# Edge scores by digit masks and one maximum, with one 16-plane load of edge numbers and three score buffers

## The reference

```
xp    = layernorm(x) @ W                       # 3125 x 1024, as 4 heads of 256
a_src = sum over a head's 256 of xp * att_src  # 3125 x 4
a_dst = sum over a head's 256 of xp * att_dst  # 3125 x 4
e     = leaky_relu(a_src[src] + a_dst[dst], 0.2)   # one row of 4 per edge
alpha = softmax of e over the edges of one dst
out   = relu(sum over a dst's edges of xp[src] * alpha + bias)
x     = x + out;   x = x + expert_layer(layernorm(x))
```

## Time and profile before

| | |
|---|---|
| median of 3 runs | 2159.19 us (2158.75 to 2162.96) |
| span of the profiled execution | 2296.1 us |
| what lies around that span | not shown |
| PE busy, its weight loads | 1959.2 us (85%), 1318.7 us (57%) |
| VectorE busy | 1470.6 us (64%) |
| ScalarE, GpSimd busy | 1137.3 us (50%), 768.2 us (33%) |
| DMA | 490.15 MB, mean 213 GB/s |
| score stage | 332 to 483 us |

### The profile page before, as it was taken

How to read it: one execution, slowest core, us unless ns; L and a number is a source line. 1 busy time by engine, 2 the same in 40 slices (tenths; PEclk the granted TensorE clock), 3 DMA queues, 4 the chain that set the end, 5 groups by cost and what they waited for, 6 DMA issues and landing times. The chain is left out here.

```text
span 2296.1 us, 53233 instructions
## 1 busy us (share of the span) xinstructions
PE 1959.2 (85%) x14846; PEld 1318.7 (57%) x14847; DVE 1470.6 (64%) x4341; ACT 1137.3 (50%) x2499; POOL 768.2 (33%) x943
## 2 busy tenths in 40 slices
PE   6999977667878888888888589983899999999997
PEld 4666545645766667777667455652454445555553
DVE  7988859987666666666666699867543443443333
ACT  4444421113666666676666566654543443443332
POOL 1020000022555555555555232321233333333332
PEclk9999976568999999999999889995899999999999
DMA  7444544403988888888888677746646556644542
GB/s 272 134 143 136 172 131 172 186 0 114 312 281 291 286 299 287 294 296 287 287 298 294 235 249 240 228 142 234 233 169 249 212 167 239 221 160 171 176 162 80
DMA packets 135664, 490.15 MB, mean 213 GB/s; under 512 B 16900, under 2 KB 17108, under 8 KB 133410
## 3 DMA queue, kind: packets, MB, share of 16 engines
q0 software_dynamic: 95568, 334.62, 43.5%
q1 hardware_dynamic: 31954, 125.15, 15.1%
q10 hardware_dynamic: 8064, 29.36, 3.7%
HBM read 419.17 MB, written 81.17 MB: 218 GB/s over the span
## 5 line engine op out<-in xcount | busy, mean ns | idle before, releaser
L1130 PE MATMUL main_ps<-rows,O 128*128 128x256 f16 x4992 | 619.2, 283 | 125.7 <-DVE acc L1066 66.3
L1113 ACT ACTIVATE O<-O,pk 128x128 f16<-128x128 f16 x1664 | 502.9, 387 | 246.1 <-DVE O L1083 203.5
L1130 PEld LDWEIGHTS main_ps<-rows,O 128*128 128x128 f16 x4992 | 480.9, 102 | 217.9 <-issue 72.8
L1052 POOL DMA_INDIRECT rows<-projected,idx x416 | 395.5, 951 | 325.2 <-PE small_ps L1135 202.9
L1087 DVE TENSOR_SCALAR O<-O,pk 128x128 f16<-128x128 f16 x1664 | 314.6, 273 | 15.0 <-issue 0.2
L1837 PE MATMUL x_h<-w_p,gram 128*128 x1344 | 307.1, 386 | 18.4 <-ACT gram L1787 7.6
L1852 PE MATMUL x_o<-w_p,gram 128*128 x1344 | 308.0, 379 | 1.4 <-ACT gram L1806 1.4
L1886 PE MATMUL pj_ps<-gram,xsT 128*125 128x512 f16 x1200 | 271.1, 385 | 8.8 <-ACT xsT L402 5.5
L1837 PEld LDWEIGHTS x_h<-w_p,gram 128*128 128x128 f16 x1344 | 131.6, 99 | 171.6 <-issue 31.5
L1886 PEld LDWEIGHTS pj_ps<-gram,xsT 128*125 128x125 f16 x1200 | 163.2, 139 | 104.7 <-ACT xsT L402 8.6
L1083 DVE TENSOR_SCALAR O<-iota,pk 128x128 f16<-128x128 f16 x416 | 109.4, 263 | 164.9 <-PE small_ps L1135 124.1
(11 more groups left out here) (346 smaller groups left out, 2538.9 us busy)
## 6 DMA issues: line engine op xcount, KB each, us to landing
w_f<-in_L_ffn_W_dram SPq DMA_DIRECT2D x14, 2048.0 KB
b_t<-in_L_ffn_b_dram ACTq DMA_DIRECT2D x56, 512.0 KB
projected_f<-xp_f POOLq DMA_DIRECT2D x25, 500.0 KB, 3.7
projected<-xp POOLq DMA_DIRECT2D x25, 500.0 KB, 4.6
out_dram<-n_x SPq DMA_DIRECT2D x25, 500.0 KB
x_after_gnn_normed<-PK POOLq DMA_DIRECT2D x25, 500.0 KB, 9.1
xt<-in_x_dram SPq DMA_DIRECT2D x24, 512.0 KB, 3.3
n_own<-projected_f SPq DMA_DIRECT2D x24, 512.0 KB, 13.0
```

The source lines that it names most:

```text
L1052: pool.indirect_dma_start(out=rows[:, 4 * p + k, :, :].rearrange("k n d -> k (n d)"), out_offset=None, in_=xp_d[:, :], in_offset=bass.Indi ...
L1113: ins = act.activation(O[:, k, 1 + HEADS + h, :], O[:, k, 0, :], ACT.Copy, scale=pk[:, p, k, w:w + 1])
L1130: pe.matmul(main_ps[:, h * C:(h + 1) * C], O[:, k, 1 + HEADS * a + h, :], rows[:, 4 * p + k, b, h * C:(h + 1) * C], start=first and h % 2 ...
```

## The change

A source is now split in base 112: `high = src // 112` (28 values, `HI`) and `low = src % 112`. `high` itself is split into `tens = high // 7` and `ones = high % 7`. Of the 128 rows of a one-hot column, 112 stand for `low`, 8 for `tens` and 8 for `ones`. The matrix that PE multiplies with (`terms`, 128 rows, 28 x 4 columns, two parts) holds the node terms in rows 0 to 111, and in the 16 rows below them a mask: 0 where a column's digit is the row's, -65504 elsewhere. The product is thus the edge's term in the right place, and a number near -65504 or lower in the 27 others, and one maximum over the 28 places finds it.

- `edge_numbers` makes three number rows (`low`, `tens`, `ones`) beside the local dst; SP stores them as 16 planes of DRAM: `low` 14 times, then `tens` and `ones`. A chunk's load copies each plane to 8 partitions (`load_numbers`), and VectorE compares each partition with its own number `src_row`.
- `digit_mask` (at block 16) makes `src_row`, a shifted identity and the mask, in 18 VectorE instructions (3 for the identity, 4 for `src_row`, 9 for the mask's values, 2 copies). After the last block PE puts the mask and the shifted node terms into `spread_ps` (about 50 small matmuls), and VectorE copies it to `terms`.
- `high_one_hots` and the turned row `hiT` are gone, and so are `pick` and the product at L790.
- There are three buffers of score sums; PE waits until the reduction of the group three before is done, where it waited for the product of the group two before.
- All eight chunks are written out on PE.

```
-HI = -(-NODES // P)
+LOW, TENS, DIGITS = 112, 7, 8
+HI = -(-NODES // LOW)
+MASK = -65504.0
...
+        def load_numbers(sp, lo, dl, vs, done):
+            sp.dma_start(lo, numbers_d[:, vs, :].rearrange("n v k -> n (v k)").unsqueeze(1).broadcast_to([P // DIGITS, DIGITS, CHUNK * P])).then_inc(done, 16)
+            sp.dma_start(dl, dloc_d[vs, :].partition_broadcast(P)).then_inc(done, 16)
...
-                            sp.dma_start(lo_d.rearrange("(p r) n -> p (r n)", r=4), rowV[:, 0, :]).then_inc(s_vstore, 16)
+                            lows = LOW // DIGITS
+                            sp.dma_start(numbers_d[0:lows].rearrange("n (p r) k -> p n (r k)", r=4),
+                                         rowV[:, 0, :].unsqueeze(1).broadcast_to([VP, lows, ROW4])).then_inc(s_vstore, 16)
+                            sp.dma_start(numbers_d[lows:].rearrange("n (p r) k -> p n (r k)", r=4), rowV[:, 2:4, :]).then_inc(s_vstore, 16)
...
-                        dve.scalar_tensor_tensor(fV[:, 2, :], fV[:, 1, :], -float(ROWS), fV[:, 0, :], ALU.mult, ALU.add)
+                        dve.scalar_tensor_tensor(rowV[:, 0, :], fV[:, 1, :], -float(LOW), fV[:, 0, :], ALU.mult, ALU.add)
+                        link(dve.tensor_scalar(fV[:, 2, :], fV[:, 1, :], 1.0 / TENS, -0.5 * (TENS - 1) / TENS, ALU.mult, ALU.add))
+                        link(dve.tensor_scalar(fV[:, 2, :], fV[:, 2, :], WHOLE, None, ALU.add))
+                        link(dve.tensor_scalar(fV[:, 2, :], fV[:, 2, :], -WHOLE, None, ALU.add))
+                        dve.tensor_copy(rowV[:, 2, :], fV[:, 2, :])
+                        dve.scalar_tensor_tensor(rowV[:, 3, :], fV[:, 2, :], -float(TENS), fV[:, 1, :], ALU.mult, ALU.add)
...
+                    def digit_mask():
...
+                            link(dve.tensor_scalar(digits_of[:, 0, :], digits_of[:, 2, :], src_row[:, :], digit[:, 3:4], ALU.not_equal, ALU.mult))
+                        for part in range(2):
+                            dve.tensor_copy(mask[:, part, :, :], digits_of[:, 0, :].unsqueeze(2).broadcast_to([P, HI, HEADS]))
...
+                    pe.matmul(spread_ps, ident16[:, :], mask[:, :, :, :], start=True, stop=True, skip_group_check=True)
+                    for n, blocks in enumerate((range(LATE), range(LATE, BLOCKS))):
+                        pe.wait_ge(s_st16, 2 * n + 2)
+                        for b in blocks:
+                            for a in range(ROWS * b // LOW, (ROWS * (b + 1) - 1) // LOW + 1):
+                                w = P - (ROWS * b - LOW * a)
+                                ins = pe.matmul(spread_ps[0:LOW, :, a, :], shift16[0:ROWS, w:w + LOW],
+                                                st16[:, b, :].rearrange("r (n g h) -> r n g h", n=2, g=2)[:, :, 0, :],
+                                                start=False, stop=True, skip_group_check=True)
...
-                            dve.tensor_tensor(pick[:, b, :, :, :], s_ps[b][:, :, :].rearrange("k v (a h) -> k v h a", h=HEADS),
-                                              hi_oh[:, four(n), :].unsqueeze(2).broadcast_to([P, 4, HEADS, HI]), ALU.mult).then_inc(s_sel, 1)
-                        dve.tensor_reduce(sT[:, four(n), :], pick[:, b, :, :, :], AX.X, ALU.add).then_inc(s_got, 1)
+                            dve.tensor_reduce(sT[:, four, :], s_ps[b][:, :, :].rearrange("k v (a h) -> k v h a", h=HEADS), AX.X, ALU.max).then_inc(s_got, 1)
...
-                            if not early(n, 2):
-                                pe.wait_ge(s_sel, n - 1)
+                            if n >= 3:
+                                pe.wait_ge(s_got, n - 2)
...
-                                    pe.matmul(s_ps[(p + q) % 2][:, u, :].rearrange("k (a h) -> k a h", h=HEADS), lo_b[p][0:ROWS, 4 * q + u, :],
-                                              st16[:, :, h0:h0 + HEADS], start=(part == 0), stop=(part == 1))
+                                    pe.matmul(s_ps[n % 3][:, u, :], lo_b[p][:, 4 * q + u, :],
+                                              terms[:, part, :, :].rearrange("r a h -> r (a h)"), start=(part == 0), stop=(part == 1))
...
-                    steps(pe, 8, body)
+                    for i in range(8):
+                        body(i, i // 2, i % 2)
```

More of the change, by code:

```diff
@@ L179, in program @@
     own_d = dram("projected_f32", (NODES, D))
[L180 removed]
+    numbers_d = dram("src_numbers_by_visit", (P // DIGITS, VISITS, P), F16)
     x2n_d = dram("x_after_gnn_normed", (NODES, 2 * D), F16)
@@ L226, in program @@
         early_ctx = ExitStack()
-        hiT = sbuf(early_ctx, "hiT", [P, VISITS], F16)
-        hi_oh = PK[:, :, :].rearrange("k v n -> k (v n)").bitcast(U8)[:, 0:VISITS * HI].rearrange("k (v a) -> k v a", a=HI)
+        src_row = sbuf(early_ctx, "src_row", [P, 1])
+        terms = sbuf(early_ctx, "src_terms", [P, 2, HI, HEADS], F16)
         dstV = sbuf(early_ctx, "dstV", [VP, ROW4])
@@ L254, in program @@
             fV = cut(VP, 8 * ROW4, 4 * ROW4, None).rearrange("v (n a) -> v n a", n=4)
-            rowV = cut(VP, 12 * ROW4, ROW4, F16).rearrange("v (n a) -> v n a", n=2)
+            rowV = cut(VP, 6 * ROW4, 2 * ROW4, F16).rearrange("v (n a) -> v n a", n=4)
+            shift16 = sbuf(c, "shift16", [P, 3 * P], F16)
+            digit = sbuf(c, "digit", [P, 4])
+            digits_of = sbuf(c, "digits_of", [P, 3, HI])
+            mask = sbuf(c, "mask", [P, 2, HI, HEADS], F16)
+            s_spread = sem("ed_spread")
             cnt = sbuf(c, "cnt", [98, BLOCKS - 1])
@@ L660, in _ @@
                     lo_proj(BLOCKS - 1)
+                    dve.wait_ge(s_spread, 1)
+                    dve.tensor_copy(terms[:, :, :, :], spread_ps)
                 @block.tensor
@@ L765, in load @@
                             sp.wait_ge(s_grp, GR * (i - 1))
-                        for t, d in ((lo_b, lo_d), (dl_b, dloc_d)):
-                            sp.dma_start(t[p], d[CHUNK * i:CHUNK * (i + 1), :].partition_broadcast(P)).then_inc(s_row[p], 16)
+                        load_numbers(sp, lo_b[p], dl_b[p], slice(CHUNK * i, CHUNK * (i + 1)), s_row[p])
                     for i in range(1, 8):
@@ L784, in body @@
                             n = GR * i + q
[L785 to L788 removed]
+                            b = n % 3
                             dve.wait_ge(s_grp, n + 1)
[L790 to L802 removed]
+                            four = slice(4 * n, 4 * n + 4) if isinstance(n, int) else bass.ds(4 * n, 4)
+                            dve.tensor_reduce(sT[:, four, :], s_ps[b][:, :, :].rearrange("k v (a h) -> k v h a", h=HEADS), AX.X, ALU.max).then_inc(s_got, 1)
                     dve.memset(Msim_f[:, 2 * KD * NX:], 0.0)
@@ L859, in body @@
                                 skip_runtime_bounds_check_because="the table counts the borders at or below a visit, of which there are BLOCKS - 1")
-                            if not early(n, 2):
-                                pe.wait_ge(s_sel, n - 1)
+                            if n >= 3:
+                                pe.wait_ge(s_got, n - 2)
                             for u in range(4):
                                 for part in range(2):
-                                    h0 = 2 * HEADS * part
-                                    pe.matmul(s_ps[(p + q) % 2][:, u, :].rearrange("k (a h) -> k a h", h=HEADS), lo_b[p][0:ROWS, 4 * q + u, :],
-                                              st16[:, :, h0:h0 + HEADS], start=(part == 0), stop=(part == 1))
+                                    pe.matmul(s_ps[n % 3][:, u, :], lo_b[p][:, 4 * q + u, :],
+                                              terms[:, part, :, :].rearrange("r a h -> r (a h)"), start=(part == 0), stop=(part == 1))
                             if not early(n, 2):
```

68 lines of the change are left out of this document (34 added, 34 removed).

## The result

The changed kernel took 2183.32 us in the median of four runs (2180.51 to 2185.37), the kernel before 2161.07 beside it (four runs): a ratio of 1.0105, 95% interval [1.0086, 1.0124], 22 us slower. The forecast was 2145.5, in a range to 2162.

A forecast was written before the change was run, and what follows sets the result against it. VectorE was taken to bound the score stage, with load landing close beside it. Gains of 3.1, 5.7 and 4.9 us sum to 13.7, the projection counts 0; off the 2159.19 us median that gives 2145.5, range 2136 to 2162.

The forecast's parts named there:

- (d): Score stage, chunks 2 to 6: load-bound, landing unchanged at 11.3 us, period 16.8 us against 17.94; 5.7 us gained.
- Slow planes: Rival: a 16-plane load source runs at half rate, landing 4.3 us later in six chunks; 12 us slower, 2171; chance 0.15.
- (b): Score stage, PE: eight matmuls of 112 columns take 0.92 us a group, bounds 0.51 and 1.10, slower than VectorE.
- (c): Score stage: with three buffers PE does groups 9 to 11 during the build, stopping before group 12.
- (e): Score stage, chunks 0 and 1: next load issued about 355.0, chunk 1 load-bound to 372.2 against 375.31; 3.1 us gained.
- (f): Score stage, chunk 7, which has no build: 12.8 us against 17.75; 4.9 us gained.
- (g): Projection, edge numbers: 2.1 us more VectorE work against 0.27 us of cover, so PE stalls 1.8 us.
- (h): Projection, digit mask: 18 small VectorE instructions, 3.7 us, bounds 2.5 and 6; PE stalls another 1.2 us.
- (i): Projection: eight high one-hots of 1.50 us each go, winning 3.4 us in four blocks.
- (j): Projection's last blocks: VectorE's wait for chunk 0's load grows when early, and PE's 4.11 us stall stays.
- (k): Projection: third turned row goes; the 16-plane store before an input load costs nothing, uncovered 5 us.
- (l): After the last block: spread matmuls and terms copy cost nothing behind GpSimd's drain; 0.5 us if it were gone.

The follow-up runs named there:

- e1: Kernel before, with only the source of the numbers load written as 16 by 8 equal rows, not 128; 2185.95 us against 2159.55, ratio 1.0123.
- e8: Changed kernel, 16-plane load kept, with the next chunk's one-hots built one reduction later, ahead of the tenth; 2156.77 us, ratio 0.9975.
- e5: Changed kernel, numbers loaded as 128 equal rows of plane 0, the two digits laid over the last 16 rows by two more transfers; 2170.09 us, ratio 1.0047.
- e6: e5 with the next chunk's one-hots built one reduction later, ahead of the tenth; 2146.06 us, ratio 0.9930.
- e13: Changed kernel with the numbers kept in 32 planes, each loaded to four rows, not 16 to eight; 2163.02 us, ratio 1.0020.
- e14: e13 with the build ahead of the tenth reduction and the first build at block 24; 2137.98 us, ratio 0.9899.
- e2: Changed kernel, numbers load reading plane 0 for all 128 partitions as equal rows, digits left out of the computation; 2148.61 us, ratio 0.9941.
- e3: Kernel before, with PE's eight chunks written out instead of a loop for the last six; 2160.33 us, ratio 1.0001.
- e16: e7 with three planes stored in the place of 16; 2129.60 us, ratio 0.9882.
- e7: e6 with the first chunk's one-hots built two blocks later in the projection, at block 24 not 22; 2133.26 us, ratio 0.9881.

## Why the prediction was wrong

The step that failed is in (d): "I take the landing unchanged: the bytes and the 128 rows of 13 KB are the same". The dst load landed 15.4 us after its issue, issued 0.57 us behind the first: 16.0 us in all against the 11.3 taken. 4.7 us in each of six chunks is 28 us, and e1 gives 26 us for the same edit alone. The sentence argued from bytes, row length and full engines; the engines were full (share 0.99), at 220 to 230 GB/s in the place of 399. The rival *Slow planes* had the slow load and its size (4.3 us a load, 25.8 in all), at a chance of 0.15; its reason, two engines that write where one did, no run here shows. Its total, 2171, is 12 us short of the result, since the rest below did not pay as reckoned. The Trainium skill, page "DMA: Bandwidth & Descriptors", section "The descriptor swizzle", gives the port that each engine writes for one transfer to 128 partitions. No run here shows a port; what the chip does with a source of 16 by 8 is known here by rate and landing alone.

By the other steps:
- (a) Right. A reduction takes 0.62 us (row at 401.80).
- (b) Right, a little low: PE's groups start 0.90 to 1.05 apart, 0.96 in the mean from 402.47 to 407.27; 0.92 was taken.
- (c) Right, and costlier than seen: PE stops before the last group, 9.62 us. That the closed loop could be opened by moving the build one reduction on, the prediction's own chain contained and did not draw. It is worth 27.3 us of stage from the changed kernel to e8, 25.5 from e5 to e6 and 16.3 from e13 to e14, each more than the 13.7 forecast for the whole change.
- (d) The rest of the sum stands. With the landing as before, e2's period is 17.5 and not 16.8; its dst median is 11.5 with a minimum of 11.3, so the 11.3 in all was 0.6 us too small.
- (e), (f) Chunk 7 from its first group to the end of the last reduction runs from 488.84 to 502.10 us, 13.3 against 12.8, which is the longer group of (b). Chunks 0 and 1 fell with the landing; in e2, where it is fast, they last 22.3 and 17.4 us, and by (e) 22.3 and 17.2.
- (g) Right: PE's stall at block 14 is 1.81 us, 1.8 was said. (h) The mask's 18 instructions take 209.79 to 213.01, 3.2 us against 3.7, PE stalls 0.65 us. (i) Right: the turns of blocks 18 to 22 come 11.25 us apart without a stall, and 4.4 us are won from block 17 to 22 (56.45 us against e3's 60.85) where 3.4 were said.
- (j) Wrong by the same step: "this stall stays", and it is 8.67 us (row at 295.76), since this load has the same shape. With a plain load it does stay: 3.89 in e2, 3.71 in e3.
- (k) Wrong, small: the store was taken for nothing. VectorE waits 2.07 us for `x` behind it at 195.19; e16 gives 1.7 us for it.
- (l) Not contradicted: the 52 small matmuls sum to 3.0 us, most of them ahead of the last block's end, and the copy takes 0.38 us at 327.03, before GpSimd's last store is issued at 327.41.

Put together: the stage lasts 166.9 us against 151.0 in e3, 16 us; it starts 5 us later than e3's, which together is 21 of the 22 us. The 5 are the larger stall: up to the turn of block 22 what digits, store and mask cost and what the one-hots give back cancel (275.68 against 275.43 in e3).

## What to carry to other kernels

Where a period is a chain of load, build and release, write the chain down and ask which link can be overtaken by reordering, before pricing the links: one instruction group moved behind one reduction was worth 16 to 27 us of stage, more than was forecast for the change. It also lowered the price of a slow load, from 27.7 us to 16.8, and did not remove it. Treat the form of a transfer's source as a thing with a price of its own, and time it in the unchanged kernel (e1 is a two-line edit) rather than argue from its bytes. A store on a queue that also feeds the main loop costs what its issue holds the queue, and in these runs that was longer the more pieces stood ahead of it (below).

## What the hardware showed beyond expectation

- 128 equal rows of 13,312 B land in 6.8 us (median) written as 32 by 4, 6.6 as 64 by 2, 6.4 and 7.0 plain (before and e3), and 10.7 as 16 by 8; while the load runs the engines are as busy in e1 (share 0.97) as in the kernel before (1.02), at 213 GB/s in the place of 399. Each packet takes 1.0 us in the place of 0.5.
- SP's issue of a load is itself longer in two steps: 0.52 us against 0.32, also in the fast 32 by 4 form.
- The issue of a store of 28 planes (2912 pieces of 1 KB) behind x loads returns at once, but the next issue, of 208 pieces, took 14.89 us, with 14 planes ahead of it 2.4 us, and with one 0.4 us (e16): the time shows at the instruction behind the large one.
- TensorE's clock mattered little in the score stage. In e7 at 2.4 GHz a group's eight products take 0.55 us, at 1.2 GHz 0.91, but the groups start 0.9 to 1.05 us apart in both, since at the higher clock each waits 0.22 us on issue (timeline of PE in e7):

```profile
399.89 0.55 PE L903 MATMUL s_ps<-src_terms,stage 128*128 128x112 f16 x8 [0.23 <-issue]
...
400.80 0.55 PE L903 MATMUL v_ps<-src_terms,stage 128*128 128x112 f16 x8 [0.22 <-issue]
401.85 0.55 PE L903 MATMUL s_ps<-src_terms,stage 128*128 128x112 f16 x8 [0.22 <-issue]
```
